# First attention of a two-layer kernel: mask on GpSimd, values in one addition, rests a slot later; ternary network: the rows' parts moved off VectorE

## The reference, cut to what matters

```python
# first attention, 16 heads of 16
dot = jnp.einsum('bhid,bhjd->bhij', q, k)
vals = q_norm_sq + k_norm_sq.transpose(0, 1, 3, 2)
scores = dot * dot / (vals - 2.0 * dot + EPSILON) * SCORE_SCALE
mask = jnp.triu(jnp.ones((Lq, Lq), dtype=scores.dtype), k=1) * -1000000000.0
attn = jax.nn.softmax(scores + mask[None, None, :, :], axis=-1)
out = jnp.einsum('bhij,bhjd->bhid', attn, v)
# ternary network
h = jax.nn.gelu(_ternary_linear(x, w_up), approximate=False)
return _ternary_linear(h, w_down)     # w_up 1024 x 256, w_down 256 x 1024
```

## Time and profile before

| | |
|---|---|
| median of 3 runs (lowest to highest) | 2969.86 us (2965.78 to 2971.8) |
| the profiled execution's own time | 2970.16 us |
| its span in the trace | 2968.4 us |
| granted TensorE clock, mean of the span | 0.981 of full |
| TensorE, VectorE, ScalarE, GpSimd busy | 2716.5, 2343.9, 2035.4, 1751.4 us |
| first attention, first to last score product of VectorE (L692) | 45.1 to 1297.4 us |
| ternary network, first rest of the rows (L1970) to the end | 2575.1 to 2968.4 us |

### The profile page before, as it was taken

One profiled execution on the slowest core, in us unless ns is written; L12 is line 12 of the kernel. 1 busy time (PEld: TensorE's weight loads), 2 busy tenths in 40 slices (PEclk: granted clock), 3 DMA queues, 4 the chain that ended last, 5 costly groups with the idle time before them and its releaser, 6 DMA issues. The chain is left out here.

```text
span 2968.4 us, 76585 instructions
## 1 busy us (share of the span) xinstructions
PE 2716.5 (92%) x28474; PEld 1933.1 (65%) x28516; DVE 2343.9 (79%) x6131; ACT 2035.4 (69%) x3686; POOL 1751.4 (59%) x3054
## 2 busy tenths in 40 slices
PE   5999999999999999977996899999999999699998
PEld 3777777777777777752333667777777777466666
DVE  5999999999999999856555677676777676499998
ACT  4999998999999999952432555555555555467776
POOL 3766667676766677745111555655565555466664
PEclk9999999999999999988997999999999999799999
DMA  4433344443333443310002645454454543000001
GB/s 110 75 66 68 66 70 76 75 74 66 67 65 68 71 75 69 68 46 8 1 1 58 104 77 88 80 85 86 79 92 78 91 74 61 1 15 22 22 22 36
DMA packets 110386, 182.29 MB, mean 61 GB/s; under 512 B 27008, under 2 KB 96384, under 8 KB 97920
## 3 DMA queue, kind: packets, MB, share of 16 engines
q1 hardware_dynamic: 106560, 176.61, 32.7%
q10 hardware_dynamic: 3456, 0.79, 0.2%
HBM read 116.25 MB, written 60.29 MB: 59 GB/s over the span
## 5 line engine op out<-in xcount | busy, mean ns | idle before, releaser
L792 POOL TENSOR_TENSOR ratio_scores<-ratio_scores,ratio_max_cols 128x512 f32<-128x512 f32 (+3 forms) x1024 | 730.3, 730 | 318.3 <-DVE ratio_max_cols L702 314.2
L1188 ACT ACTIVATE zeroed_prob<-bank 128x512 f32<-128x512 f32 x640 | 376.6, 593 | 291.3 <-PE bank L1078 197.5
L1295 DVE TENSOR_REDUCE zeroed_max_cols<-bank 128x1 f32<-128x512 f32 (+3 forms) x1024 | 441.7, 481 | 158.2 <-PE bank L185 156.9
L182 PE MATMUL bank<-ratio_k_stack,ratio_q_stack 102*128 102x512 bf16 (+7 forms) x2048 | 508.3, 303 | 29.9 <-DVE ratio_max_cols L702 13.3
L702 DVE CUSTOM_DVE_ANT_0 ratio_scores<-bank,ratio_scores 128x512 f32<-128x512 f32 (+3 forms) x1024 | 472.5, 489 | 22.2
L564 ACT ACTIVATE ratio_prob<-bank 128x512 f32<-128x512 f32 x640 | 380.1, 594 | 106.0 <-PE bank L478 105.8
L692 DVE TENSOR_TENSOR ratio_scores<-bank,ratio_inverse 128x512 f32<-128x512 f32 x640 | 435.8, 681 | 17.3 <-PE bank L182 10.2
L475 PE MATMUL bank<-const_f_sb,ratio_scores 128*128 128x128 f32 x2560 | 409.9, 274 | 0.7 <-ACT ratio_prob L564 0.7
L1404 POOL TENSOR_SCALAR_AFFINE_SELECT zeroed_prob<-zeroed_prob 128x256 f32<-128x256 f32 (+1 forms) x640 | 227.5, 365 | 288.1 <-ACT zeroed_prob L1188 286.2
L553 ACT ACTIVATE ratio_inverse<-bank 128x512 f32<-128x512 f32 x640 | 382.6, 598 | 13.0 <-PE bank L185 12.5
L185 PE MATMUL bank<-const_b_sb 128*128 128x128 bf16 x2048 | 387.3, 221 | 0.0
(11 more groups left out here) (169 smaller groups left out, 5354.1 us busy)
## 6 DMA issues: line engine op xcount, KB each, us to landing
ratio_q_stack<-ratio_parts_q SPq DMA_DIRECT2D x186, 128.0 KB
ratio_k_stack<-ratio_parts_k SPq DMA_DIRECT2D x186, 128.0 KB
zeroed_q_stack<-zeroed_parts_q SPq DMA_DIRECT2D x186, 128.0 KB, 4.5
zeroed_k_stack<-zeroed_parts_k SPq DMA_DIRECT2D x186, 128.0 KB, 7.5
ratio_parts_q<-ratio_parts SPq DMA_DIRECT2D x96, 128.0 KB
ratio_parts_k<-ratio_parts SPq DMA_DIRECT2D x96, 128.0 KB
zeroed_parts_q<-zeroed_parts SPq DMA_DIRECT2D x96, 128.0 KB
zeroed_parts_k<-zeroed_parts SPq DMA_DIRECT2D x96, 128.0 KB
```

The lines of the kernel that those rows point to most:

```text
L182: i = e.matmul(bank[:, off:off + w], qs[0:rows, s, hh, ib * P:(ib + 1) * P], ks[0:rows, s, hh, 0:w], start=(k == 0), stop=mask is None, sk ...
L792: i = e.tensor_tensor(seg, seg, mx[:, pair % M_BUFS, c:c + 1].to_broadcast([P, w]), ALU.subtract)
L1188: e.activation(prob[:, n % FOLD_PROBS, 0:wd], exp_banks[n % 2][:, 0:wd], ACT.Exp, scale=0.25).then_inc(s["prob"])
L1295: i = e.tensor_reduce(mx[:, pair % FOLDS, c:c + 1], bank[:, off:off + (ib + 1) * P], AX_X, ALU.max)
```

## The change: what it does

- The mask of the first attention's scores is no longer added by TensorE in `turn`. GpSimd writes -1e9 into the masked places of the diagonal blocks with one select for each slot (`mask(n - 1)`, in slot n behind `less(n)`), and `turn` waits for that and only transposes. The mask table leaves the constants.
- The values of a half are projected into one bank in slot 9 and get their bias in one addition, where they were projected in two steps with two additions each.
- The other steps of `prepare` (q, k and norms) stand one slot later on VectorE (`SPLIT_LAG`) and two slots later on GpSimd, counted from the slot in which TensorE and ScalarE do theirs.
- In the ternary network VectorE keeps the rows' rest alone. The middle part is copied by ScalarE and the low part subtracted by GpSimd, at f = 3 and 6.

```diff
-PREP_AT = ({2: "q", 4: "k", 6: "n", 9: "va", 12: "vb", 16: "x0"}, {0: "x1", 2: "q", 4: "k", 6: "n", 9: "va", 13: "vb"})
+PREP_AT = ({2: "q", 4: "k", 6: "n", 9: "v", 16: "x0"}, {0: "x1", 2: "q", 4: "k", 6: "n", 9: "v"})
+SPLIT_LAG = 1
...
             def turn(n):
                 bank = exp_banks[n % 2]
-                q.wait_ge(s["lessened"], n + 1)
+                q.wait_ge(s["masked"], n + 1)
                 q.wait_ge(s["prob"], n - 1)
-                first = True
-                for _, ib, off in UNITS[n % N_UNITS]:
-                    wd = (ib + 1) * P
-                    for jb in range(ib + 1):
-                        at = slice(off + jb * P, off + (jb + 1) * P)
-                        e.matmul(bank[:, at], scores[:, n % S_BUFS, at], net.ident,
-                                 is_transpose=True, start=first, stop=False, skip_group_check=True)
-                        first = False
-                    i = e.matmul(bank[:, off + wd - P:off + wd], net.ident_b, net.mask(B_SCORE),
-                                 start=False, stop=True, skip_group_check=True)
+                for t in range(T):
+                    at = slice(t * P, (t + 1) * P)
+                    i = e.transpose(bank[:, at], scores[:, n % S_BUFS, at], net.ident)
                 i.then_inc(s["turned"])
...
-                for tt in range(2):
-                    i = e.tensor_tensor(values_ones[:, half % 2, 2 * pair + tt, :, 0:HD], by_head(shared("prep", use)[:, tt * P:(tt + 1) * P]),
-                                        by_head(w.bias_v[:, m * P:(m + 1) * P]), ALU.add)
-                i.then_inc(s["prep_read"])
+                e.tensor_tensor(values_ones[:, half % 2, :, :, 0:HD], by_head(shared("prep", use)[:, :]),
+                                bias.unsqueeze(1).to_broadcast([P, T, HALF, HD]), ALU.add).then_inc(s["prep_read"])
...
-                step = ratio_prep_at(n, halves)
-                if step:
+                step, late = ratio_prep_at(n, halves), ratio_prep_at(n - SPLIT_LAG, halves)
+                if late and late[2] != "v":
+                    prepare(*late)
+                if step and step[2] == "v":
                     prepare(*step)
...
+            def mask(n):
+
+                blocks = [off // P + ib for _, ib, off in UNITS[n % N_UNITS]]
+                to = scores[:, n % S_BUFS, :].rearrange("p (k t) -> p k t", k=T)
+                diagonal = to[:, blocks[0]:T:max(blocks[-1] - blocks[0], 1), :]
+                q.wait_ge(s["lessened"], n + 1)
+                e.affine_select(diagonal, diagonal, [[0, 2]][:len(blocks) - 1] + [[-1, P]], ALU.is_ge, dropped, 0, 1).then_inc(s["masked"])
...
                 if n < total:
                     less(n)
-                step = ratio_prep_at(n, halves)
+                if 0 < n <= total:
+                    mask(n - 1)
+                step = ratio_prep_at(n - 2 * SPLIT_LAG, halves)
...
+            def middle_x(b, pair):
+                q.wait_ge(s["x_rest"], 2 * b + pair + 1)
+                q.wait_ge(s["up"], (b - 1) * FC)
+                e.activation(x_part(b, pair, 1), x_rest[:, :, :], ACT.Copy).then_inc(s["x_mid"])
...
-                q.wait_ge(s["x_rest"], at + 1)
-                e.tensor_copy(part(1), x_rest[:, :, :]).then_inc(s["x_mid"])
-                q.wait_ge(s["x_mid"], at + 1)
-                e.tensor_tensor(part(2), x_rest[:, :, :], part(1), ALU.subtract).then_inc(s["x_lo"])
...
+            def low_x(b, pair):
+                q.wait_ge(s["x_mid"], 2 * b + pair + 1)
+                q.wait_ge(s["up"], (b - 1) * FC)
+                e.tensor_tensor(x_part(b, pair, 2), x_rest[:, :, :], x_part(b, pair, 1), ALU.subtract).then_inc(s["x_lo"])
```

More of the change, by code:

```diff
@@ L286, in ratio_prep @@
 def ratio_prep(b, what):
-    order = ["x0", "x1"] + [f"{k}{m}" for m in range(2) for k in ("q", "k", "n", "va", "vb")]
+    order = ["x0", "x1"] + [f"{k}{m}" for m in range(2) for k in ("q", "k", "n", "v")]
     return len(order) * b + order.index(what) + 1
@@ L340, in ratio_shared_uses @@
     halves = total // HALF_UNITS
-    order = [("prep", ratio_prep(0, what)) for what in ("x0", "x1", "q0", "k0", "n0", "va0", "vb0")]
+    order = [("prep", ratio_prep(0, what)) for what in ("x0", "x1", "q0", "k0", "n0", "v0")]
     order += [("denoms", n) for n in range(DENOM_LEAD)]
@@ L510, in prepare @@
                     norm_rows(2 * b + m)
-                if what[0] == "v":
-                    values(2 * b + m, "ab".index(what[1]))
+                if what == "v":
+                    values(2 * b + m)
             turn_x(0, 0)
@@ L518, in pe @@
             norm_rows(0)
-            values(0, 0)
-            values(0, 1)
+            values(0)
             for n in range(DENOM_LEAD):
@@ L1857, in ternary_feed_forward @@
         summed = lambda n: (n // FC) * (FC - 1) + n % FC
+        x_part = lambda b, pair, k: x_parts[:, b % 2, k, :, pair * 256:(pair + 1) * 256]
         def pe(q):
@@ L1955, in act @@
                     keep_x(b + 1, T_TURN_AT.index(f))
+                if b + 1 < B and f in T_PARTS_AT:
+                    middle_x(b + 1, T_PARTS_AT.index(f))
                 if b and f == T_SUMS_AT:
@@ L2059, in pool @@
                     e.tensor_tensor(total[:, b % 2, :], total[:, b % 2, :], sq[:, n % 2, :], ALU.add).then_inc(s["h_summed"])
+                if b + 1 < B and f in T_PARTS_AT:
+                    low_x(b + 1, T_PARTS_AT.index(f))
         def sp(q):
```

39 lines of the change are left out of this document (20 added, 19 removed).

## The result

The changed kernel takes 3057.78 us (median of 4 runs, 3056.13 to 3065.23) beside 2967.82 us for the kernel before: 1.0307 times as long, 95% interval 1.0285 to 1.0329. The forecast was 2915 us. The change is slower by 90 us, in a way that none of the rivals held whole.

The account below looks back on a forecast made before the run. VectorE was taken to set the first attention's pace. Gains there of 62 + 9 + 5 - 29 - 5 = 42 us, plus 13 us in the ternary network, gave 2970.2 - 55 = 2915 us; range 2880 to 2960 us.

Parts of the forecast that it names:

- Gain: 55.1 x 1.13 = 62 us.: First attention: VectorE's wait for ScalarE's squares disappears when the rests run one slot later, 62 us gained.
- I cost it at nothing; without that cover it would be 64 x 0.7 = 45 us.: First attention: k's projection waits some 0.7 us longer for its bank; hidden, cost 0, otherwise 45 us.
- The gather ... cost 0, at most 31 x 3 = 93 us.: First attention: gathers come 4 us later, TensorE waits 1 to 2 us a half, hidden by three slots of lead.
- rival (d): Slower by the gather: its 4 us are not hidden, VectorE loses 2 us in 31 halves, 2977 us; 7%.
- 64 + 32 = 96 conversions: 29 us lost.: First attention: VectorE's moved conversions meet GpSimd's subtractions, 0.3 us each, 29 us lost (0 to 103).
- Rival (c): Slower by port waits: each of 96 conversions meets a full GpSimd subtraction, 103 us in place of 29, 2989 us; 8%.
- I take half, 5 us (bounds 0 and 10): First attention: score mask moved to GpSimd sheds TensorE products, shortening VectorE's waits for TensorE by 5 us.
- gain 9 us: First attention: four value additions of 31 us in all become 32 of 0.689 us, 22 us; 9 us gained.
- no wait is charged (0 to 0.5 us each, 16 us): Values' addition: TensorE's 8 products in one slot cause no wait, as two VectorE slots lie between.
- Four engines near full: First attention: with none more than a tenth free, engines take time from each other, 5 us lost (0 to 40).
- Ternary network: 13 us gained.: Ternary network: 20 us of TensorE's waits go, about 7 us return; net 13 us, between 31 gained and 10 lost.
- What was to show it.: Trace signs named beforehand for a right or wrong forecast, including the first attention's stage 40 us shorter.

Follow-up runs that it names:

- lag_1_1: Kernel before with rests on VectorE and low parts on GpSimd both one slot later: 2971.97 us, ratio 1.0013.
- lag_alone: Kernel before with only the lag: rests one slot later on VectorE, low parts two slots later on GpSimd; 3042.99 us, ratio 1.0264.
- mask_dummy: Kernel before, TensorE's mask products kept, with GpSimd's 640 selects added on a spare tile nothing reads: 2982.24 us, ratio 1.0053.
- low_late: Kernel before with low parts two slots later on GpSimd and nothing later on VectorE: 3135.81 us, ratio 1.0567.

## Why the prediction was wrong

**"Gain: 55.1 x 1.13 = 62 us."** This step failed. The wait for squares did vanish, but it was no gain to be had. VectorE was read as the one engine that sets the pace, and TensorE, 1085 us busy, as one with room. In the slots of this wait it has none: TensorE spends 1.98 us on a projection in one queue with the score products, and behind it VectorE waits for the next product with or without the squares. To this come the projection of k and the norms, which wait for the later rest. Removed were 55.1 us; in their place came 40.7 us of waits for products and 15 us of longer casts (lag_1_1).

**"I cost it at nothing; without that cover it would be 64 x 0.7 = 45 us."** The size was right for the whole of the new waits for products, 40.7 us in the stretch and 46 us over the stage, but by luck. The mechanism it names, a bank that is read late, accounts for the waits in slots 5 and 7, 0.61 us a half or 20 us. Half of the new waits, 0.71 us a half or 23 us, stand in slot 3 behind the projection of q, which waits for no rest; that TensorE's own work would fill the place of the wait stands in no step. The cover named, that the product is wanted two slots later, was not there: `dots(n)` may start only once the maxima of slot n - 2 are done, and one projection of 1.98 us uses that lead up. The 8.1 us of the earlier trace rows showed that TensorE is late at times, though in slots 18 and 19.

**What was missing: one tile for the rest.** The low part's wait for the tile, 28.1 us in the stretch and 34 over the stage (x 640 / 525), stands in no step. With the diff q's low part stands in slot 4 on GpSimd, behind that slot's subtraction and a select, and k's rest in slot 5 on VectorE; from that alone the two meet.

**"The gather ... cost 0, at most 31 x 3 = 93 us."** The wait itself was forecast at 1 to 2 us in each half; it is 1.5 to 3.0 us in every second one. That it would be hidden was wrong: rival (d) priced it at 2 us of VectorE in each of 31 halves, 62 us, and the gather accounts for 44 of the 79 us of lag_alone. The margin was read in the earlier trace rows from a gather made in a long half (8.0 us from issue to use in the mean), the easier kind; in the short ones it is 6.1 us.

**"64 + 32 = 96 conversions: 29 us lost."** Right in size: 10 + 17 = 27 us. But the ports' largest price, 39 us, fell on the layer norm's pass, which the change doesn't touch and the sum therefore left out. Rival (c) has the right kind of mechanism on the wrong instructions, and it charges at most one subtraction, where the long passes sat through runs of six and seven instructions.

**"I take half, 5 us (bounds 0 and 10)" for the mask.** The relief is 9 us, within the bounds, and the selects cost 16. The forecast took only GpSimd's time as their price and looked whether it fits there, which it does: no turned score waited for a select that mattered (0.2 us). What it didn't take was the time of VectorE beside them, and that the selects close the gaps between GpSimd's subtractions.

**Values: "gain 9 us", "no wait is charged (0 to 0.5 us each, 16 us)".** Measured is a loss of 14 us by the medians and of 10 by the two traces of the stage (1252 and 1262 us). The wait is there, 11.5 us for 28, 0.41 us each, near the upper end. In the stretch the additions save 27.1 - 19.4 = 7.7 us of listed time. From one score product to the next, slot 9 takes 0.70 us more in each half and slots 12 and 13 together 0.40 us less, 32 x 0.30 = 10 us lost. With the low parts one slot late and the mask off TensorE, the same step costs too little to be told (0.9969 [0.9958, 0.9981] with it, 0.996 [0.9946, 0.9975] without).

**"Four engines near full", 5 us.** Nothing separate is left for this term.

**Ternary network: 13 us gained.** Right in the sum: 13 us in the trace, 12 alone. Waits of TensorE there, to be read against the earlier trace rows:

```profile
PEld bank L1890 <- DVE ternary_h_parts L1997: 1.7, 3, 0.9
...
PE bank L1890 <- DVE ternary_h_parts L1997: 0.7, 2, 0.4
```

Its terms were off in ways that cancel. TensorE's products wait 14.0 us less for the hidden values' low parts, where 20 were booked. The rows' last part is waited for only at the first blocks (5.9 us, two times, where 3.1 us stood before), so of the 6 us charged for the 15 blocks and 1 for the start, 3 were needed. GpSimd's low part takes 1.57 us, not the 1.17 assumed.

With these errors added, the sum would have come out near the result: of the 42 us of gain in the first attention, take 45 for the late products, 44 for the gather, 34 for the tile of the rest and 39 for the layer norm's pass, and 120 us of loss are left, where 100 were measured; the waits overlap, so they need not add up exactly.

**What was to show it.** No wait for squares, TensorE waiting on the gather, and L1886's waits for L1991 under 5 us came true. But behind the wait on the gather stood one of VectorE, which the forecast had ruled out. VectorE at 95% of the stretch did not come true (89%), nor did the parts' cast at 0.6 to 0.9 us in the median (0.50), and the sign named for a wrong forecast, waits of the product L692 on TensorE in their place, is the largest row of VectorE's waits.

## What to carry to other kernels

A wait on an engine is worth its length only as far as the engine that feeds it would deliver sooner. For the moment at which the wait begins, look when the feeder's next output is ready: here 0.7 of 1.79 us were the feeder's own work. Then look for what the feeder itself waits for, and delay that on paper before the gain is booked. When a step is moved late on one engine, go through every wait that the step's outputs and its single buffers release, and price the move at the tightest of the repeated cases, not at the first one found; here halves of two lengths alternate. Work given to GpSimd is also paid by VectorE's untouched casts and tensor_scalar passes beside it, most where it closes the gaps between GpSimd's instructions; count them.

## What the runs showed of the hardware

GpSimd's selects, at 85% busy (947 of 1120 us in mask_dummy), raise the mean length of a 128x256 float32 tensor_scalar pass of VectorE from 610 to 1110 ns. Nearly all of that is 12 passes of 2.8 us, which end 0.15 us after a run of six GpSimd instructions without a gap. Products that read PSUM stay at 680 to 682 ns, and statistics passes that read SBUF at 415 to 416 ns.

After a wait of 2.33 us TensorE's products run longer for a while: the 102-row product is listed with 0.61 us at 638.12 and with 0.38 us at 643.29. The granted clock in between (third number from the right: 0.50, which is 1.2 GHz) is half of the full one, which is back at 643:

```profile
638.00:640.00 2.00, 1.88 (x26) 1.12 (x26) 0.64 (x4) 0.60 (x1) 1.28 (x2) 0.50 0.09 29
```

Such stretches make 24 of the 1120 us in the changed kernel and none in the kernel before. By an estimate from these numbers they cost at most half of their length, 12 us of the stretch. In low_late, whose waits are longest (4.3 us), the mean granted clock of the stretch is 0.95.
